# A GRU beside a mixture of experts: the scatters of a pair of chunks one to a planned step, fewer idle products, and the addition's two waits in the other order

## What is computed

```python
def cell(h, x):
    gi = x @ W_ih + b_ih
    gh = h @ W_hh + b_hh
    i_r, i_z, i_n = jnp.split(gi, 3, axis=-1)
    h_r, h_z, h_n = jnp.split(gh, 3, axis=-1)
    r = jax.nn.sigmoid(i_r + h_r)
    z = jax.nn.sigmoid(i_z + h_z)
    n = jnp.tanh(i_n + r * h_n)
    return (1.0 - z) * n + z * h
...
probs = jax.nn.softmax(x @ w_gate, axis=-1)            # x: hidden rows
topk_w, topk_ids = jax.lax.top_k(probs, 2)
topk_w = topk_w / jnp.sum(topk_w, axis=-1, keepdims=True)
...
gu = jnp.einsum('th,ehf->etf', x, w_gate_up)           # 8 experts, 256 wide
eo = jnp.einsum('eti,eih->eth', _silu_and_mul(gu), w_down)
routed = jnp.einsum('te,eth->th', combine, eo)
shared = _silu_and_mul(x @ w_sh_gate_up) @ w_sh_down   # 1024 wide
return x + (routed + shared)
```

## Time and profile before

| | |
|---|---|
| median of 3 runs | 1250.64 us (1248.44 to 1251.01) |
| the profiled execution | 1243.78 us, span 1241.9 us |
| granted TensorE clock, mean | 0.989 of full |
| PE | 1041.9 us busy (84%), 13472 matmuls |
| DVE | 861.0 us (69%) |
| ACT | 573.5 us (46%) |
| POOL | 206.1 us (17%), 213 instructions |
| idle products, L838 | 258, 47.1 us busy |
| additions, L1598 | 55, 88.4 us busy |
| scatters, L1591 | 32, 32.0 us busy |

### The profile page before, as it was taken

The page is one execution under the profiler, slowest core; times in us unless marked ns, Lnnn a source line. Parts: engine busy times, 40 slices in busy tenths (PEclk is TensorE's granted clock), DMA queues, the critical chain, the costliest instruction groups (busy, mean ns, idle before and its releaser), DMA issues.

```text
span 1241.9 us, 35936 instructions
## 1 busy us (share of the span) xinstructions
PE 1041.9 (84%) x13472; PEld 625.9 (50%) x13472; DVE 861.0 (69%) x4089; ACT 573.5 (46%) x1877; POOL 206.1 (17%) x213
## 2 busy tenths in 40 slices
PE   2789887778998898899889989997998888788874
PEld 2556555455654455455545545554545444454542
DVE  5898888688888786777777767777777777611111
ACT  5755555555454443344435434443444443425442
POOL 0100100201011212111211121112111222223332
PEclk9899999999999999999999999999999999999998
DMA  8923554638164641722362326232514253569673
GB/s 304 418 75 100 206 209 161 126 123 304 36 246 153 197 145 20 262 87 44 36 213 78 53 27 220 72 61 71 202 29 146 36 152 123 181 219 281 194 234 55
DMA packets 66911, 183.15 MB, mean 147 GB/s; under 512 B 7738, under 2 KB 40289, under 8 KB 59169
## 3 DMA queue, kind: packets, MB, share of 16 engines
q1 hardware_dynamic: 45632, 107.74, 24.2%
q0 software_dynamic: 21104, 73.11, 22.9%
HBM read 137.01 MB, written 52.87 MB: 153 GB/s over the span
## 4 chain that ended last, share of the span: by engine, by line
PE 45%; DVE 26%; DMA 12%; issue 8%; ACT 8%; POOL 0%; POOLq 0%; SPq 0%; ACTq 0%; DVEq 0%
PE psG L702 15%; PE psG L708 14%; DMA y<-arena 8%; DVE arena L1031 5%; DVE arena L1029 5%; PE psU L765 4%; ACT arena L1413 3%; ACT arena L1409 3%; DVE arena L1053 3%; DVE arena L1039 3%; DVE arena L1041 3%; DVE arena L1049 3%; PE psG L838 3%; PE psD L777 2%; DVE arena L1033 2%
## 5 line engine op out<-in xcount | busy, mean ns | idle before, releaser
L702 PE MATMUL psG<-arena 128*32 128x384 f16 x4096 | 214.4, 330 | 95.8 <-DVE arena L1053 87.0
L1409 ACT ACTIVATE arena<-arena 128x32 f32<-128x32 f32 x256 | 58.5, 229 | 354.9 <-DVE arena L1033 347.0
L708 PE MATMUL psG<-arena 128*32 128x384 f16 x4096 | 215.1, 327 | 5.8 <-issue 5.7
L765 PE MATMUL psU<-arena 128*128 128x256 f16 (+1 forms) x1920 | 201.5, 252 | 0.9 <-issue 0.6
L1029 DVE STREAM_TRANSPOSE arena<-psG 128x128 f32<-128x128 f32 x256 | 81.0, 316 | 173.7 <-PE psG L708 168.6
L702 PEld LDWEIGHTS psG<-arena 128*32 128x32 f16 x4096 | 86.3, 96 | 194.6 <-DVE arena L1053 156.2
L765 PEld LDWEIGHTS psU<-arena 128*128 128x128 f16 x1920 | 157.1, 98 | 50.2 <-issue 14.2
L1598 POOL DMA_INDIRECT y<-arena x55 | 88.4, 1606 | 399.1 <-ACT arena L1506 172.7
L708 PEld LDWEIGHTS psG<-arena 128*32 128x32 f16 x4096 | 110.8, 97 | 65.1 <-issue 8.9
L809 PE MATMUL psS<-arena 128*128 128x512 f16 x468 | 116.5, 379 | 15.9 <-DVE arena L1253 10.6
L1031 DVE STREAM_TRANSPOSE arena<-psG 128x256 f32<-128x256 f32 x256 | 104.0, 406 | 0.0
(11 more groups left out here) (162 smaller groups left out, 1598.3 us busy)
## 6 DMA issues: line engine op xcount, KB each, us to landing
arena<-expert_weights SPq DMA_DIRECT2D x39, 1536.0 KB, 9.1
arena<-wgu POOLq DMA_DIRECT2D x32, 512.0 KB, 6.0
expert_weights<-arena POOLq DMA_DIRECT2D x9, 1536.0 KB, 5.6
gi_scratch<-arena SPq DMA_DIRECT2D x84, 128.0 KB, 3.1
arena<-gi_scratch SPq DMA_DIRECT2D x14, 768.0 KB, 7.3
arena<-wd POOLq DMA_DIRECT2D x16, 512.0 KB, 6.1
arena<-x SPq DMA_DIRECT2D x8, 512.0 KB, 3.7
hidden_rows<-arena SPq DMA_DIRECT2D x16, 256.0 KB
```

The costliest lines, as they stand in the source:

```text
L702: e.matmul(psG[32 * j:32 * j + 32, 0:384], prev[:, c, 2:6].rearrange("p q n -> p (q n)"), whv[c][1][:, :, :, 32 * j:32 * j + 32], start=(c ...
L708: r = e.matmul(psG[32 * j:32 * j + 32, 0:384], prev[:, c, 0:4].rearrange("p q n -> p (q n)"), whv[c][0][:, :, :, 32 * j:32 * j + 32], star ...
L765: r = e.matmul(psU[u % 2][:, 256 * gu:256 * gu + width], half(W_GS + ex * 4 + c, pw)[:, o:o + 128], hh[:, 1 - ph, c, first:first + width], ...
L1409: e.activation(Ur, Ur, ACT.Tanh, scale=reg_tr).then_inc(th_r, 1)
```

## The change

Three edits. `file(g)` becomes two or four pieces `file(g, j)` of the plan, chained, at a cost of 3.0 each for a pair group, so that the planner places one in a step; `record` two groups on and `rows` follow the last piece. The budget that `warm` fills up falls from 1.7 to 1.45 us. An addition's waits are written in the other order: `added` first, then `s_ev` or `e_ev`.

```diff
@@ -235,8 +235,9 @@
         listed = [("list", i, 0) for i in range(STATIC) if group_of(i) == g - 1]
         p.add("PE", ("counts", g), 0.15 + 0.15 * n, [("choose", g)], due=due, takes=True)
         p.add("DVE", ("rank", g), 0.95 + 0.2 * n, [("counts", g), ("choose", g)] + listed, due=due, frees=True)
-        p.add("DVE", ("record", g), 1.0, [("rank", g), ("route_w", g)] + ([("file", g - 2)] if g > 1 else []), due=due)
-        p.add("POOL", ("file", g), 1.3 * 2 * n, [("record", g), ("rows_init", 0)], due=due)
+        p.add("DVE", ("record", g), 1.0, [("rank", g), ("route_w", g)] + ([("file", g - 2, 2 * len(GROUPS[g - 2]) - 1)] if g > 1 else []), due=due)
+        for j in range(2 * n):
+            p.add("POOL", ("file", g, j), 3.0 if n == 2 else 1.3, [("file", g, j - 1)] if j else [("record", g), ("rows_init", 0)], due=due)
 
     for u in range(US):
         n = u % 8
@@ -278,7 +279,7 @@
             first = s - 2 if BOUND[i] <= SINGLE else s - 38
             for part, cost in enumerate(costs):
                 p.add("DVE", ("list", i, part), cost, before if part == 0 else [("list", i, part - 1)], due=first + 0.1 * part)
-            p.add("POOL", ("rows", i), 1.0, [("list", i, 0 if i == STATIC else 2), ("file", group_of(i))] + ([("rows_turn", i - 1)] if i else []), due=first + 1)
+            p.add("POOL", ("rows", i), 1.0, [("list", i, 0 if i == STATIC else 2), ("file", group_of(i), 2 * len(GROUPS[group_of(i)]) - 1)] + ([("rows_turn", i - 1)] if i else []), due=first + 1)
             p.add("PE", ("rows_turn", i), 0.4, [("rows", i)], due=first + 1, takes=True)
             p.add("DVE", ("rows_out", i), 0.45, [("rows_turn", i), ("scales", 1)], due=first + 1, frees=True)
         due = s + 4 + (7.0 if i < 4 else 4.0) * (k - FIRST_BLOCK[i])
@@ -883,7 +884,7 @@
                     else:
                         down(*n)
                 if 2 < t < T - 1 and PLAN.load("PE", t) < 1.2:
-                    warm(t, int((1.7 - PLAN.load("PE", t)) / 0.165))
+                    warm(t, int((1.45 - PLAN.load("PE", t)) / 0.165))
 
         @block.vector
         def _(e):
@@ -1583,23 +1584,23 @@
                 last = 256 * b + 256 if b < NBLK - 1 else NTOK + DUMP
                 e.dma_start(y[256 * b:last, :], xt[256 * b:last, :]).then_inc(st_y[b % 2], 16)
 
-            def file(g):
-                e.wait_ge(recorded, g + 1)
-                if g == 0:
-                    e.wait_ge(st_rows, 16)
-                for j in range(2 * len(GROUPS[g])):
-                    e.indirect_dma_start(row_d[:, :], by(slot[g % 2][:, j:j + 1]), rec[g % 2][:, j], None).then_inc(filed[g % 2], 16)
-
-            def add_rows(index, out, no):
+            def file(g, j):
+                if j == 0:
+                    e.wait_ge(recorded, g + 1)
+                    if g == 0:
+                        e.wait_ge(st_rows, 16)
+                e.indirect_dma_start(row_d[:, :], by(slot[g % 2][:, j:j + 1]), rec[g % 2][:, j], None).then_inc(filed[g % 2], 16)
+
+            def add_rows(index, out, no, ready, v):
+                need(e, added, 16 * no)
+                e.wait_ge(ready, v)
                 if no == 0:
                     for k in range(2):
                         e.wait_ge(st_y[k], 16 * (NBLK // 2))
-                need(e, added, 16 * no)
                 e.indirect_dma_start(y, by(index), out, None, compute_op=ALU.add).then_inc(added, 16)
 
             def s_add(q):
-                e.wait_ge(s_ev, q + 1)
-                add_rows(tok_u[:, q:q + 1], so[q % 2], ADDS[("s_add", q)])
+                add_rows(tok_u[:, q:q + 1], so[q % 2], ADDS[("s_add", q)], s_ev, q + 1)
 
             def rows(i):
                 K = LAST_BLOCK[i] - FIRST_BLOCK[i]
@@ -1627,8 +1628,7 @@
                 e.indirect_dma_start(hg[k % 2], None, hid_d[:, :], by(rid[:, k:k + 1])).then_inc(ld_hid[k % 2], 16)
 
             def add(k):
-                e.wait_ge(e_ev, k + 1)
-                add_rows(rid[:, k:k + 1], ob[k % 2], ADDS[("add", k)])
+                add_rows(rid[:, k:k + 1], ob[k % 2], ADDS[("add", k)], e_ev, k + 1)
 
             for t in range(PLAN.steps):
                 for kind, *n in PLAN.of("POOL", t):
```

## The result

The change made the kernel faster: medians 1250.1 us before and 1237.95 after (four runs each), ratio 0.9907 with a 95% interval of 0.9888 to 0.9926, 11.6 us (9.3 to 14.0). The forecast was 1244.8. The profiled execution after took 1236.97 us, span 1235.2.

The account below looks back on a forecast made before the run. It took the recurrence's chain of 3.80 us steps, 82% of the span, plus a 170 us tail as the bound; +7.2 - 5.9 - 3.0 - 3.3 - 0.8 = -5.8 on 1250.64 gave 1244.8 us, range 1236 to 1251.

Parts of the forecast that it names:

- the additions in the recurrence: Recurrence: 16 early additions move from 0.73 to 1.22 into the step; 15 still hold PE's signal, +7.2 us.
- The scatters: Recurrence: stalls under scatters of groups 2 and 4 shorten, -3.3 us; a clock fall behind group 4 goes, -0.8.
- The tail: After the recurrence: 13 additions start 0.49 sooner behind a landing, -6.4, one late addition +0.5; together -5.9 us.
- the lower bound: Tail: if PE and ACT come no earlier than now, the last evict limits the gain to -2.5 us.
- the 0.35 given back by each: Recurrence: each of 16 early additions delays its step by 0.35 us, returned on leaving that place; at most -5.6.
- The first rival: Recurrence: additions at 1.22 come too late to hold PE's signal; half of 16 free, +1.1 for +7.2; 1238.7 us, chance 0.20.
- Idle products: Recurrence: with 8 idle products for ten, 18 steps each lose 0.17 us of delay, -3.0 us.
- fall of the clock for want of work: Rival: with fewer idle products PE's clock falls in nearly every second of 32 steps, +11.2; 1256.0 us, chance 0.10.
- The median of before: Whole kernel: the change of -5.8, summed on a profiled execution of 1243.78 us, was applied to the median 1250.64.

Follow-up runs that it names:

- e2: Kernel before with only the additions' two waits exchanged; ratio to before 0.9923, 9.6 us (6.6 to 12.5) faster.
- held sets: Sets of runs where before takes 1245.6 to 1248.6 us and an instruction of POOL can hold back PE's signal; the result is of this kind.
- e3: Kernel before with only the idle products' budget cut from 1.7 to 1.45; ratio to before 0.9959, 5.1 us (2.4 to 7.7) faster.
- e4: Kernel before with only the scatters made pieces of the plan, waits and idle products as before; ratio to before 0.9996.
- e15: Kernel before with exchanged waits and smaller idle budget, without the pieces, in a set where before takes 1245.6 us; ratio to before 0.9910.
- e1: Kernel before, unchanged, timed against itself and profiled a second time; ratio 0.9992, profiled span 1246.9 us.
- free sets: Sets of runs where before takes 1217.4 or 1219.1 us and hardly any instruction of POOL holds back PE's signal.
- e12: The changed kernel again, in a set where before takes 1219.1 us; ratio to before 0.9943.
- e11: Kernel before with exchanged waits and smaller idle budget, without the pieces, in a set where before takes 1219.1 us; ratio to before 0.9937.
- e9: Changed kernel with each scatter waiting for PE's signal of its planned step, in a set where before takes 1219.1 us; ratio to before 0.9922.
- e8: The changed kernel again, in a set where before takes 1217.4 us; ratio to before 0.9928, recurrence 989.3 us.

## Why the prediction was wrong

The sign was right, the size was half of what was measured: -5.8 against 11.6 us less. The step that failed is the additions in the recurrence, put at +7.2 and measured near nothing. The scatters' -4.1, also near nothing, hid part of that error. By its steps, with the terms of the sum:

- **The tail, -5.9: right in mechanism, about right in size.** 0.27 behind a landing, as said. The tail took 167.6 to 168.1 us in three profiles of before, and 160.6 after and 161.0 in e2: -7. With the other unpaced traces of the held sets it is less: the old order has 166.4 in e3 and 165.5 in e4, the new one 160.5 in e15, and the means are 6.4 apart. The chain that ended last is DMA for 12% of the span on the page of before and 4% after (above), for in the last stretch it now runs over PE, its evicts and one landing. So the tail came to be bound by PE, as the lower bound had it, but PE and the evicts had come forward: the last evict of a block ends at 1222.55, 4.6 earlier than in the earlier trace rows, where that bound had held it still.
- **The additions in the recurrence, +7.2: the step that failed.** It read the place 1.22 off a single scatter and took 15 of 16 as held. In e2 six are held by 0.6 to 0.8 and the others at that place lose 0.1 or less, in the changed kernel eight are; with the 0.35 given back by each, the term is -1.3 in e2 and +0.6 in the changed kernel by the first profile of before (7.4 against 6.8; -0.1 against e1's 7.5). The addition behind group 7's scatters, left out of these sums, lost 0.4 more in both. Two additions both 1.26 into a step come out 0.70 apart, so one row couldn't tell the price of a place. The trace of before had rows against it. Timeline of before, the first scatter of group 3:

```profile
604.35 0.19 DVE L1053 SCALAR_TENSOR_TENSOR arena<-arena 128x32 f16<-128x32 f32 x1
605.63 0.99 POOL L1591 DMA_INDIRECT expert_rows<-arena  x1 [9.31 <-DVE arena L1171]
606.23 0.32 DVE L1029 STREAM_TRANSPOSE arena<-psG 128x128 f32<-128x128 f32 x1 [0.48 <-PE psG L708]
```

It starts 1.28 into its step, 0.03 behind that of the earlier trace rows, and L1029 is 0.10 late, not 0.82; the first scatters of all six pair groups are like it, 1.28 to 1.30 in and 0.10 to 0.13 late. The first rival, that a part of the additions doesn't hold the signal, was the right mechanism (though not for its reason, that they come too late). Its 1238.7 is close to the 1237.95 in part by luck, for it holds the -4.1 of the scatters too.

- **Idle products, -3.0: right.** The 18 steps are back at 3.81, and e3 alone gave 5.1 (2.4 to 7.7). No fall of the clock for want of work. The Trainium skill's rule ("TensorE: Matmul & The Clock Gate", section "What's actually happening"), that the granted clock follows recent activity, isn't contradicted. All falls between the first and last step in the held traces stand behind a stall under scatters. But eight products or ten made no difference to it that these traces show. In the free sets the few windows at half clock in the recurrence stand at long steps too: at 245.2 in e12 behind a step of 5.46 us, at 246.9 and 424.4 in e11 behind one of 6.05 and in one of 5.28, at 884.9 in e9 behind 2.26 us in which PE waited for a gather. A stall doesn't always bring one: e8 has a step of 5.16 us at 239.8 and no fall.
- **The scatters, -3.3 and -0.8: wrong, 0 measured** (e4). That POOL isn't paced by steps was read rightly; that the shift of an addition would shorten two stalls held for one. Group 4's three steps take 13.2 us in the changed kernel and 13.3 in e4, where they took 15.3 in the first profile of before and 14.5 in e1, as forecast. Group 2's take 16.1 and 16.0 where they took 14.8 and 14.7: it kept its 7 us with three scatters behind the addition, got a step of 5.08 behind, and in the changed kernel the clock fell for 10.2 us. Where falls come differs from one profile to the next of the same kernel: two, two and three windows in the recurrence of before, at 234.5 and 732.9, at 620.5 and 856.0, and at 239.7, 495.7 and 734.7.
- **The median of before.** The sum was made against a profile of 1243.78 us and carried over to 1250.64. Three profiles of before have recurrences of 1018.1, 1022.7 and 1018.9 us, a mean of 1019.9: the sum was made against one that is 1.8 under it, and carried the whole gap to the median over unchanged.

With measured terms: -6.4 to -7 tail, +0.3 to +1.0 additions (with the one behind group 7), -3.0 idle products, 0 scatters: -8.4 to -9.7, at the near end of the 9.3 to 14.0 measured or just under it. What the rest is stays open; windows at half clock, which come at other places in each profile, are one candidate that no run separates.

## What to carry to other kernels

A cost per planned step only spaces work out on an engine that waits for the step; on one that runs ahead, pieces of a plan without a wait of their own stand as close as before. Before pacing anything, look at the place in the step at which an instruction of POOL starts: here the stalls under the six pair groups were gone, 20.7 us to 0.5, once each scatter waited for the signal that it would have held. And don't price a place in a step from one row, when the same trace has others at that place. When two semaphores guard one DMA, the one that comes last should be the DMA's own, here worth 0.49 us each time.

## What the runs showed that I had not expected

- The same instruction order, with the same durations on POOL (1.0 us a scatter, 1.6 an addition), holds PE's products and its signal in some sets and hardly at all in others: 1018.4 and 989.3 us of recurrence for the changed kernel, as much as the 28 us between the sets' medians of before.
- Additions at the same place in a step, 1.26 in, cost 0.80 and 0.10. Which are held is the same in 17 of 18 and in 16 of 16 cases in other traces of the held sets, so something other than the place decides, and no run shows what.
- An addition that starts 2.54 to 2.70 into a step costs 0.1 to 0.3 us also in the free sets, where one at 1.26 costs nothing.
